# Attention pass of a graph network: TensorE sums both halves of a pair of half-blocks at the head of the next turn

## What is computed

```python
xh = (h @ W).reshape(n, H, C)                       # H = 4 heads, C = 32
alpha = leaky_relu(a_src[src] + a_dst[dst], 0.2)
alpha = exp(alpha - segment_max(alpha, dst)[dst])
denom = segment_sum(alpha, dst)
out = segment_sum(xh[src] * alpha[:, :, None], dst) / denom
```

## Time and profile before

| what | value |
|---|---|
| median of 3 runs | 14096.02 us (14094.08 to 14115.67) |
| the profiled execution's own time | 14089.3 us |
| its span | 14087.1 us |
| mean granted TensorE clock | 0.584 |
| attention pass, first gather's start to last gather's start | 6781.3 to 8950.4 us |

### The profile page before, as it was taken

One profiled execution on the slowest core, in us unless ns is written; L12 is line 12 of the kernel. 1 busy time (PEld: TensorE's weight loads), 2 busy tenths in 40 slices (PEclk: granted clock), 3 DMA queues, 4 the chain that ended last, 5 costly groups with the idle time before them and its releaser, 6 DMA issues. The chain is left out here.

```text
span 14087.1 us, 101802 instructions
## 1 busy us (share of the span) xinstructions
PE 6019.7 (43%) x27042; PEld 4715.8 (33%) x27043; DVE 3432.9 (24%) x6131; ACT 1003.5 (7%) x1981; POOL 9588.9 (68%) x9490
## 2 busy tenths in 40 slices
PE   3444444333343444444344444664444446333333
PEld 2333333333333222232243433332222223333333
DVE  4222222111111222222344444351112224111111
ACT  1000000000000000000000000041111112000000
POOL 1777776777776666667577777307777771677777
PEclk9555555555555555555556556586676667555555
DMA  3222222222222222222233333223333332222222
GB/s 98 53 53 53 54 53 49 53 53 54 53 54 50 59 61 61 61 61 62 65 78 78 78 78 78 68 81 96 95 95 95 93 94 82 73 59 60 60 61 57
DMA packets 518282, 956.11 MB, mean 68 GB/s; under 512 B 173581, under 2 KB 327634, under 8 KB 516604
## 3 DMA queue, kind: packets, MB, share of 16 engines
q0 software_dynamic: 301056, 623.59, 17.9%
q1 hardware_dynamic: 217120, 331.46, 7.6%
HBM read 846.72 MB, written 107.67 MB: 68 GB/s over the span
## 5 line engine op out<-in xcount | busy, mean ns | idle before, releaser
L739 POOL DMA_INDIRECT work<-rows_a,index x4704 | 4644.8, 987 | 1742.5 <-issue 1533.1
L768 PE MATMUL psum<-onehot,work 128*128 128x80 f32 x12544 | 2634.4, 405 | 4251.7 <-DMA work<-rows_a,index 3045.6
L768 PEld LDWEIGHTS psum<-onehot,work 128*128 128x128 f32 x12544 | 2549.9, 314 | 4357.2 <-issue 4357.1
L1390 POOL DMA_INDIRECT regionC<-attention_rows,index x1568 | 1692.4, 1079 | 568.5 <-issue 477.6
L903 POOL DMA_INDIRECT work<-rows_b,index x1568 | 1666.3, 1063 | 582.5 <-issue 501.4
L739 POOL DMA_INDIRECT work<-rows_b,index x1568 | 1539.3, 982 | 541.4 <-issue 522.2
L975 PE MATMUL psum<-regionB,onehot 128*80 128x256 f32 x3136 | 910.8, 462 | 1235.5 <-ACT regionB L952 1235.5
L826 DVE TENSOR_TENSOR regionA<-regionA,psum 128x80 f32 x784 | 185.6, 237 | 4744.0 <-PE psum L768 4742.5
L975 PEld LDWEIGHTS psum<-regionB,onehot 128*80 128x80 f32 x3136 | 574.9, 187 | 1543.7 <-issue 1413.6
L182 POOL COPY work<-regionB 128x500 f32 (+1 forms) x75 | 45.2, 603 | 1040.6 <-DVE regionB L648 1040.6
L1036 DVE TENSOR_TENSOR regionB<-work,regionB 128x2048 f32<-128x2048 f32 x98 | 225.4, 2300 | 1727.8 <-DMA work<-rows_b,index 1727.8
(11 more groups left out here) (338 smaller groups left out, 6527.9 us busy)
## 6 DMA issues: line engine op xcount, KB each, us to landing
regionB<-in_edge_attr SPq DMA_DIRECT2D x195, 512.0 KB, 4.4
work<-rows_a,index POOLq DMA_INDIRECT x4704, 2.5
work<-rows_b,index POOLq DMA_INDIRECT x3136, 2.5
work<-edge_columns SPq DMA_DIRECT2D x98, 512.0 KB
regionC<-attention_rows,index POOLq DMA_INDIRECT x1568
x_transposed<-regionA SPq DMA_DIRECT2D x75, 250.0 KB, 6.1
rows_a<-regionC SPq DMA_DIRECT2D x50, 250.0 KB
h_transposed<-regionB SPq DMA_DIRECT2D x50, 250.0 KB, 2.4
```

Source lines behind the costliest of these rows:

```text
L739: pool.indirect_dma_start(rows3[h][:, t, :], None, table, bass.IndirectOffsetOnAxis(ap=net.index[:, k, h * ST + t:h * ST + t + 1], axis=0) ...
L768: last = nc.tensor.matmul(bank_of(h, q, 0), rows3[h][:, t, :], onehot[:, h * ST + t, :], start=(k == 0), stop=(k == GT - 1))
L1390: pool.indirect_dma_start(ring[s][:, t, :], None, net.XH, bass.IndirectOffsetOnAxis(ap=net.index[:, k, t:t + 1], axis=0)).then_inc(gathere ...
```

## The change

TensorE takes the sums of half 1 of the pair before directly behind those of half 0, at the head of the turn. The lift of half 1 stays at the turn's end. The order of the other engines' streams and all semaphores stay as they are.

```diff
                     t.then_inc(windows, 1)
                     if not first:
                         sums_of(pe.snap(n - 1), (s + 2) % 3, 1 - k, 0)
+                        sums_of(pe.snap(n - 1), (s + 2) % 3, 1 - k, 1)
                     pe.wait_ge(blocks_ready, n + 2)
                     pe.wait_ge(ends_ready, n + 1)
@@
                     if not first:
-                        sums_of(pe.snap(n - 1), (s + 2) % 3, 1 - k, 1)
                         lift(pe.snap(n - 1), 1)
```

## The result

The changed kernel took 14144.3 us in the median of ten runs, the kernel before 14103.4 in ten. The ratio of the runs (of their means; the medians alone give 1.0029) is 1.0026, 95% interval 1.0018 to 1.0035: the changed kernel is slower by 0.26%, some 37 us, where 0.23% was forecast. The profiled execution took 14144.8 us, its span is 14142.6, 55.5 more than before. The three parts of that difference: until the first gather of the attention pass 11.2 us (6781.3 to 6792.5), in stages that are the same code; from the first to the last gather's start 38.5 (2169.1 to 2207.6); behind it 5.8. Only the middle part is the change's: the first is spent ahead of the pass, and from the last gather's start to the pass's last add it took 41.2 us before and 40.4 after.

The account below looks back on a forecast made before the run. GpSimd's unbroken chain of gathers was taken as the bound. Stretch of 0.41 + 0.3, taken as 0.6 us, times 48 turns is 29 us, plus 3 for the last turn: +32, giving 14128 us, range 14083 to 14152.

Parts of the forecast that it names:

- The bound: Attention pass: GpSimd's 1568 gathers form a chain without a gap, 44.3 us a turn, and set the stage's length.
- The moved matmuls: TensorE's work behind the moved sums, and so messages L1729, come 0.2 to 4.3 us later, hidden by VectorE's 17 us wait.
- the clock: TensorE: more dense work ahead of L1532 should keep the clock high in most turns, L1532 nearer 3.75 than 5.9 us.
- The wait that goes: VectorE's add of half 1 no longer waits 0.78 us for lift 1; worth nothing by itself, as VectorE has slack.
- the buffer freed earlier: `packed[1]` is free for GpSimd some 12 us sooner, but no gather waits for it: 0 us.
- Term (a): Behind L1729's end (E): the compare L1594 begins earlier, so the gather under it is stretched 0.41 us more a turn.
- faster rival: At the compare L1594: it slips behind the gather, which passes free; 19 us less, 14080 us; chance 13%.
- Term (b): L1715 to L1729: VectorE instructions meet gathers at other places; stretch 2.6 us as a mean over all, 0.3 more a turn.
- The sum: Whole pass: 0.7 us a turn taken as 0.6, times 48 turns 29 us, plus 3 us once: +32 us.
- late gathers restore themselves: L1715 to L1729: the cheapest places are also where late gathers restore themselves, so 0.7 us a turn was cut to 0.6.
- The 3 us of the last turn: The last turn has no gathers to hide behind: messages up to 4.3 us later, 0.78 saved, 3 us once.
- The skill's rule: A tensor_tensor does not stall descriptor generation, so only L1646 would stretch a gather: 14099 us; chance 3%.

Follow-up runs that it names:

- changed, again: The changed kernel unaltered, run again beside the kernel before on another chip: ratio 1.0026, medians 14119.9 and 14092.1 us.
- with the memset: Changed kernel plus a dummy VectorE memset of 200 columns into an unused PSUM bank ahead of the compare L1594: ratio 1.0035 to the kernel before.
- with three transposes: Changed kernel plus three dummy TensorE transposes ahead of the matmuls of `chained`: ratio 1.0015 to the kernel before.
- window in PSUM: Changed kernel with only the second operand of the compare L1594 (the window) read from PSUM: 14043.5 us, ratio 0.9966 to the kernel before.
- both in PSUM, sums at the head: Changed kernel with the second operands of compare L1594 (window) and messages L1729 (exponentials) read from PSUM: 13925.6 us, ratio 0.9883 to the kernel before.
- both in PSUM, sums at the end: Kernel before, half 1's sums at the turn's end, with second operands of compare and messages read from PSUM: 13919.7 us, ratio 0.9877.
- all three in PSUM, sums at the end: Kernel before with second operands of compare and messages in PSUM, and mask L1646 made a tensor_tensor taking its lane from PSUM: 13881.4 us, ratio 0.9853.
- gap experiment: Changed kernel plus a dummy VectorE add (192 columns, one SBUF and one PSUM operand) ahead of the compare: 14089.2 us, ratio 0.9999 to the kernel before.

## Why the prediction was right

- *The bound.* GpSimd's issue sets the stage on the chips of 14100 us: in each experiment there the time followed L1390's busy time. The differences from the kernel before, in us, for the busy time from its profile of the earlier trace rows and for the median from its runs on the same chip:

| kernel | gathers' busy time | median |
|---|---|---|
| changed | +38.3 | +40.9 |
| changed, again | +35.9 | +27.7 |
| with the memset | +46.9 | +47.7 |
| with three transposes | +20.5 | +15.8 |
| with the filler of one SBUF operand | 0.0 | -2.2 |
| window in PSUM | -45.9 | -47.9 |
| both in PSUM, sums at the head | -168.8 | -166.6 |
| both in PSUM, sums at the end | -163.8 | -171.7 |
| all three in PSUM, sums at the end | -203.7 | -210.0 |

- *The moved matmuls.* Hidden, as said. In the turn shown, from the first sums to L1729 passed 17.42 us before and 17.88 in the turn above: 0.46 us later, near the low end of 0.2 to 4.3. But the kernel before has two kinds of turns, and the prediction counted from one alone. In 25 of the 47 turns between the first and the last L1532 took 5.8 to 5.9 us and L1729 came 19.2 to 19.4 us behind ScalarE's copy (L1452); in 22 L1532 took 3.75, at a granted clock of 1.00 throughout, and L1729 came after 16.5 to 16.9. One turn of the second kind, before:

```profile
7976.76 0.30 ACT L1452 COPY turn<-regionC 128x128 f32<-128x128 f32 x1 [21.98 <-DMA regionC<-attention_rows,index]
...
7993.44 4.49 DVE L1729 TENSOR_TENSOR regionC<-regionC 128x2048 f32<-128x2048 f32 x2
```

  After the change it is 19.5 to 19.8 in all turns. So L1729 came 0.4 us later in the one kind and 2.9 in the other, 1.6 in the mean, and all of it was hidden. Of the clock the prediction was right in part. In the turn shown the granted clock was 0.50 up to 7832.6 and 1.00 from 7834.2, so that the second block took some 2.5 us; but inside L1533 it fell, from 1.00 up to 7839.0 to 0.50 from 7840.5, and over the turns L1533 took 3.7 to 5.2 us: in most nearer 3.75 than 5.9, but in few at the high clock to its end.
- *The wait that goes, the buffer freed earlier.* Both worth nothing, as said.
- *Term (a), 0.41 a turn.* Over those 47 turns the stretch behind L1729 (each gather longer than 0.96 us, counted against 0.944) rose from 1.99 to 2.40 us in the mean, exactly that. A common turn pays more than said: 2.53 in place of 2.02, because the adds begin 0.03 us behind E and not 0.07 ahead of it, so that the compare comes at E + 2.24. But in every sixth, the first of a loop pass, the compare comes 0.25 us later still, the gather slips ahead and pays 1.54. So the faster rival was real, for one turn in six, and the gap experiment made it so for all. That these add up to 0.41 is luck in part.
- *Term (b), 0.3.* The stretch up to L1729 rose from 2.42 to 2.77: 0.35. But it isn't a mean over all places. After the change all turns but the last of the 47 pay 2.6 to 3.0; the spread that I averaged over doesn't exist, and the right mean was luck to that extent. The trace says what to count instead: the delay less whole steps of the gathers' rhythm. The two kinds of turns before lay 2.5 us apart, two steps of 1.249, and so met the gathers at the same place and paid the same (2.3 to 2.5 in most turns of either kind); the delays of 0.4 and 2.9 us are both 0.4 beyond whole steps, and both lead to the dear place. The 0.9 us of the three transposes filled it up to one step more, and the price was that of before.
- *The sum.* I cut 0.7 to 0.6 with the argument that late gathers restore themselves. Nothing in the traces shows such a gain: the two terms together were 0.76, some 36 us for 47 turns. The gathers rose by 38.3 where I had 29; some 5 of it (1568 x 0.003) is that an undisturbed gather took 0.947 us in this execution and 0.944 in the one before. In the repeated run it took 0.944, and the rise is 1728.3 - 1692.4 = 35.9. The 3 us of the last turn didn't come: from its first copy (L1452) to the last add it took 35.7 us before and 35.1 after, since its messages were only 0.4 us later.
- *The skill's rule.* The Trainium skill, "SBUF — State Buffer", section "Who interferes with whom", was weighed as a rival, under which a tensor_tensor wouldn't stall descriptor generation. That rival is dead: taking the second SBUF operand away from two tensor_tensors was worth 194 us. The same section's sentence that an instruction with at most one SBUF input outside the 2-port modes doesn't contend agrees with the 0.95 us gathers under L1731; whether it covers the memset that held a gather no run here shows.
- What isn't settled: what the gather does at its start and near its end that is held. The traces show only that there are two such moments: on the chips of 14100 us, a gather that begins inside L1729, the compare or the mask ends 0.82 us after the end of that instruction, if the mask doesn't hold it again; and one that would end 0.5 us or more into the mask ends 0.12 us after the mask's end, where one that would end 0.2 us into it is not held. Under L1729 and the compare alone no gather was held that late. Nor is it settled where the 17 us came from that the profiled execution lost outside the gathers, in code that is the same.

## What to carry to other kernels

Where GpSimd issues gathers without a pause, look at VectorE's long instructions that lie over them before asking what TensorE does: a move that costs nothing on its own engine can shift them by 0.4 us against the gathers' rhythm, and 47 turns of that are visible. What counts is the shift less whole steps of that rhythm. Give such instructions their second operand from PSUM: for two of them that was worth 194 us, five times the change studied here, with one more ScalarE instruction in each turn. A filler that shifts an instruction can itself be such a holder: read its own row before judging what it shifted.

## What the runs showed of the hardware that was not expected

A memset of 200 columns into PSUM, with no operand from SBUF, held a gather too: begun 0.15 us ahead of the compare, it took 3.72 us (stretch 2.78), where one that began 0.16 us ahead with no memset there took 0.94. On one chip of the three that the experiments ran on, single TensorE matmuls came with gaps of 1.0 to 1.6 us that no wait explains, and the kernels took 15416 us (before) and 15420 (changed), 9% more; the change made no difference there. And L1729 let the held gather through between its two instructions in every turn, so that the next one, begun 1.2 us into the second, cost 0.95 us each time, before and after.
